# Graph attention on one core: edges laid out as 392 consecutive ones along each partition, with a small stage that joins the partitions afterwards

## The reference, cut to what matters

```python
x = layernorm(x + L0(x, stack([src, dst])))        # 3 layers: gather rows, matmul, relu, segment_sum
q, k, v = x @ Wq + bq, x @ Wk + bk, x @ Wv + bv    # per node, 8 heads of 16
e = edge_attr @ We                                 # per edge, 64 -> 128
k_j, v_j = k[src] + e, v[src] + e
logits = sum(q[dst] * k_j, axis=-1) / sqrt(16)     # per edge and head
m = segment_max(logits, dst)                       # softmax over the edges with one target
ex = exp(logits - m[dst])
alpha = ex / segment_sum(ex, dst)[dst]
agg = segment_sum(alpha * v_j, dst)                # per node, 128
h = ln(agg + x @ Wskip + bskip + x)
x = layernorm(x + ln(gelu(h @ Wf1 + bf1) @ Wf2 + bf2 + h))
```

## Time and profile before

| | us |
|---|---|
| median of the runs | 4584.0 |
| the profiled execution, first to last instruction | 5458.0 |
| attention, first gather to last averaged row | 3201.2 to 4589.7 |

### The profile page before, as it was taken

One profiled execution on the slowest core, in us unless ns is written; L12 is line 12 of the kernel. 1 busy time (PEld: TensorE's weight loads), 2 busy tenths in 40 slices (PEclk: granted clock), 3 DMA queues, 4 the chain that ended last, 5 costly groups with the idle time before them and its releaser, 6 DMA issues. The chain is left out here.

```text
span 5458.0 us, 111849 instructions
## 1 busy us (share of the span) xinstructions
PE 4332.6 (79%) x23759; PEld 2886.3 (53%) x23858; DVE 3587.2 (66%) x12001; ACT 2141.5 (39%) x4806; POOL 2901.1 (53%) x2863
## 2 busy tenths in 40 slices
PE   5666664888867888689999967777777775999998
PEld 2444443666645666556666635555555553444444
DVE  7566653444434444478888847667766765899998
ACT  0222221444433444323333323232323332777777
POOL 0555555555535555354444335555555553777775
PEclk9888887999979999989999977777877777999999
DMA  0333334666646666568888744444544443444443
GB/s 18 125 123 131 127 126 119 189 192 186 188 139 184 188 190 189 172 195 266 266 262 264 241 154 134 131 134 130 143 132 129 135 132 92 117 125 128 126 128 99
DMA packets 693097, 852.73 MB, mean 156 GB/s; under 512 B 149445, under 2 KB 511032, under 8 KB 692916
## 3 DMA queue, kind: packets, MB, share of 16 engines
q1 hardware_dynamic: 580020, 631.94, 35.7%
q0 software_dynamic: 112896, 218.94, 16.7%
HBM read 451.91 MB, written 398.61 MB: 156 GB/s over the span
## 5 line engine op out<-in xcount | busy, mean ns | idle before, releaser
L760 POOL DMA_INDIRECT mp_gathered<-msg_rows,other_idx x784 | 752.4, 960 | 659.0 <-PE bank L776 211.1
L776 PE MATMUL bank<-mp_edge_hot,mp_gathered 128*128 128x256 bf16 x3528 | 539.7, 282 | 203.1 <-issue 166.0
L1066 POOL DMA_INDIRECT ll_gathered<-msg_rows,other_idx x392 | 376.1, 959 | 479.1 <-PE bank L1085 228.8
L526 POOL DMA_INDIRECT by_window<-so_pay,so_pos_i x392 | 397.7, 1015 | 435.5 <-issue 299.0
L1372 POOL DMA_INDIRECT at_kv<-kv_rows,kv_idx x392 | 375.6, 958 | 456.3 <-PE bank L1403 176.4
L776 PEld LDWEIGHTS bank<-mp_edge_hot,mp_gathered 128*128 x3528 | 349.8, 99 | 349.2 <-issue 294.3
L879 DVE TENSOR_TENSOR mp_msg_out<-mp_rest,mp_msg_out 128x256 bf16<-128x256 f32 x392 | 166.8, 425 | 490.5 <-ACT mp_msg_out L837 290.7
L824 ACT ACTIVATE mp_h_out<-bank,mp_b_agg 128x256 f32<-128x256 f32 x392 | 185.8, 474 | 714.5 <-PE bank L794 321.6
L1670 POOL DMA_INDIRECT ff_agg<-at_rows,last_idx x392 | 385.8, 984 | 115.9 <-issue 103.0
L1374 POOL DMA_INDIRECT at_q<-q_rows,node_idx x392 | 371.8, 948 | 130.2 <-issue 130.2
L856 DVE TENSOR_SCALAR mp_edge_hot<-digits,mp_first_col,column 128x256 bf16<-128x256 bf16 x1176 | 346.7, 357 | 80.3 <-issue 62.0
(11 more groups left out here) (258 smaller groups left out, 10199.2 us busy)
## 6 DMA issues: line engine op xcount, KB each, us to landing
msg_rows<-mp_msg_out SPq DMA_DIRECT2D x392, 192.0 KB
mp_h_in<-h_cols SPq DMA_DIRECT2D x392, 128.0 KB
h_cols<-mp_h_out SPq DMA_DIRECT2D x392, 128.0 KB
kv_rows<-ll_proj SPq DMA_DIRECT2D x98, 512.0 KB
msg_rows<-so_msg_out SPq DMA_DIRECT2D x98, 384.0 KB
h_cols<-so_h_out SPq DMA_DIRECT2D x98, 256.0 KB
ll_h_in<-h_cols SPq DMA_DIRECT2D x196, 128.0 KB
x_rows<-ll_x_b SPq DMA_DIRECT2D x98, 256.0 KB
```

The lines of the kernel that those rows point to most:

```text
L526: pool.indirect_dma_start(core.by_window, bass.IndirectOffsetOnAxis(ap=pos_i[k][:, t:t + 1], axis=0), pay[k][:, t, :], None, bounds_check= ...
L760: pool.indirect_dma_start(gathered[:, r * PARTS * D:(r + 1) * PARTS * D], None, core.msg_rows[layer % 2], bass.IndirectOffsetOnAxis(ap=cor ...
L776: product = nc.tensor.matmul(agg_bank[k], gathered[:, bass.ds(at + d * D, D)], hot, start=(first and d == 0), stop=True, skip_group_check= ...
L1066: pool.indirect_dma_start(gathered[:, r * PARTS * D:(r + 1) * PARTS * D], None, core.msg_rows[(LAYERS - 1) % 2], bass.IndirectOffsetOnAxis ...
```

## The change

Partition p now holds edges 392p to 392p+391, and group g is 4 consecutive edges of every partition. So the edges of one target lie along the free dimension without any transpose, and the state is compact: a maximum and a denominator for 8 heads (128 x 8 a step of 4, laid out as 8 x 5 with a slot in front that carries the previous group's value) instead of 128 x 512. The numerator scan is 128 x 640 (128 channels x 5 slots). `factor` holds exp of two gaps (weight and decay) for 8 heads, and ACT spreads the decay to 16 channels. POOL gathers four tiles of keys and values, waiting for `ke_ok`, then four of queries, waiting for `prod_ok`; each kind counts on its own semaphore. PE keeps only the attribute transposes, the product with We (into four PSUM banks in turn, not one) and the skip product (two banks); the fillers are gone. The flags are no longer written and loaded: they are computed once as a table in SBUF (`joins`, and from it `brk` for all groups, 128 x 3920).

The tables of the sort become 128 x 392 tables loaded directly, without four transposes. A target whose edges cross from one partition to the next is not finished by this scan. The new stage `join_runs` gathers each partition's first finished row, carries the ends across the 128 partitions with scans, and scatters the corrected rows back. So rows in `at_rows` are now 144 numbers wide (128 values, 8 maxima, 8 denominators), and `feed_forward` gathers 576 B instead of 512 B a row.

```diff
-        self.at_rows = dram("at_rows", [NP + 1, D], F32)
-        self.same_row = dram("same_row", [1, NP + 1], BF16)
+        self.at_rows = dram("at_rows", [NP + 1 + P, ROW], F32)
...
-                for c, tile in enumerate(parts_f):
-                    for b in range(T):
-                        last = nc.tensor.transpose(bank[c][:, b * P:(b + 1) * P], tile[:, b, :], core.ident[:, :])
+                nc.vector.tensor_tensor(core.joins[:, 1:NT], core.node_idx[:, 1:NT], core.node_idx[:, 0:NT - 1], ALU.is_equal).then_inc(tab, 1)
...
@@ attention, SP @@
-            def load_flags(g, k, i):
-                reached(sp, brk_ok, g - DEEP + 1)
-                sp.dma_start(same[k][:, :], core.same_row[0, bass.ds(g * GR, GR)].partition_broadcast(D)).then_inc(same_in[k], 16)
+                for lo, hi in ((0, SPLIT), (SPLIT, last)):
+                    sp.dma_start(attr[k][lo:hi, :, :], bass.AP(edge_attr.tensor, edge_attr.offset + (lo * NT + g * J) * ED,
+                                                              [[NT * ED, hi - lo], [ED, J], [1, ED]])).then_inc(a_in[k], 16)
+                sp.dma_start(core.at_rows[0:NP, :].rearrange("(p j) f -> p j f", j=NT)[:, g * J:(g + 1) * J, :],
+                             rows[g % DEEP][:, :, :]).then_inc(st[g % DEEP], 16)
@@ attention, POOL @@
-                reached(pool, prod_ok, g - DEEP + 1)
-                reached(pool, ve_ok, g - DEEP + 1)
-                reached(pool, e_mm, g - DEEP + 2)
-                for t in range(T):
...
+                reached(pool, ke_ok, g - DEEP + 1)
+                for t in range(J):
+                    at = g * J + t
+                    pool.indirect_dma_start(kv[g % DEEP][:, t, :], None, core.kv_rows,
+                                            bass.IndirectOffsetOnAxis(ap=core.kv_idx[:, at:at + 1], axis=0)).then_inc(kv_in[g % DEEP], 16)
                 reached(pool, prod_ok, g - DEEP + 1)
+                for t in range(J):
+                    at = g * J + t
                     pool.indirect_dma_start(q[g % DEEP][:, t, :], None, core.q_rows,
+                                            bass.IndirectOffsetOnAxis(ap=core.node_idx[:, at:at + 1], axis=0)).then_inc(q_in[g % DEEP], 16)
@@ attention, ACT @@
+                nc.scalar.activation(factor[k][:, :, :, 1:SLOT].rearrange("p a h j -> p (a h) j"),
+                                     gap[k][:, :, :, :].rearrange("p a h j -> p (a h) j"), ACT.Exp, scale=-SCALE).then_inc(f_ok, 1)
+                nc.scalar.activation(decay[k][:, :, :].rearrange("p (h c) j -> p h c j", h=H),
+                                     factor[k][:, 1, :, :].unsqueeze(2).broadcast_to([P, H, C, SLOT]), ACT.Copy).then_inc(dec_ok, 1)
+                nc.scalar.activation(rows[k][:, :, D:ROW], top_den[k][:, :, :, 1:SLOT].rearrange("p a h j -> p j (a h)"), ACT.Copy).then_inc(state_ok, 1)
@@ attention, DVE @@
             def turn(do):
+                do(0, values)
+                do(-1, weigh)
+                do(0, keys)
+                do(-1, num_scan)
+                do(0, products)
+                do(-1, den_scan)
                 do(0, edge_logits)
-                do(-2, weigh)
-                do(-2, num_scan)
-                do(-2, den_scan)
-                do(-1, maxima)
-                do(-3, divide)
+                do(-1, carry_num)
+                do(-1, inverses)
+                do(0, maxima)
+                do(0, gaps)
+                do(0, carry_top)
+                do(-1, averages)
...
+def join_runs(core):
...
+            pool.indirect_dma_start(firsts[:, :], None, core.at_rows, bass.IndirectOffsetOnAxis(ap=core.run_end[:, 0:1], axis=0)).then_inc(a_in, 16)
+            pool.wait_ge(row_ok, 1)
+            pool.indirect_dma_start(core.at_rows, bass.IndirectOffsetOnAxis(ap=core.run_to[:, 0:1], axis=0), firsts[:, :], None).then_inc(moved, 16)
...
+            nc.vector.tensor_tensor_scan(top[:, 1:1 + P], brk[:, :], z[:, 1, :], 0.0, ALU.add, ALU.max).then_inc(c_ok, 1)
...
+            nc.vector.tensor_tensor_scan(num[:, 1:1 + P], scale[:, 1, :], end_v[:, :], 0.0, ALU.mult, ALU.add).then_inc(c_ok, 1)
```

More of the change, by code:

```diff
@@ new lines, in attention @@
+        brk = sb("break", [P, NG * FLAT])
+        logits, top_den = two("logits", [P, H, SLOT]), two("top_den", [P, 2, H, SLOT])
+        drop, gap = sb("drop", [P, H, J]), two("gap", [P, 2, H, J])
+        factor, decay = two("factor", [P, 2, H, SLOT]), two("decay", [P, D, SLOT])
+        wv, num, inv = two("weighted", [P, D, SLOT]), two("num", [P, D, SLOT]), two("inv", [P, H, J])
+        rows, zero_rows = deep("rows", [P, J, ROW]), sb("zero_rows", [P, ROW])
+        in_run, runs = sb("in_run", [P, NT - 1]), sb("runs", [P, 8])
@@ L1354, in _ @@
+            for n in range(-5, NG + 4):
+                for lag, step in ((5, load), (3, load_cols), (-1, store_skip), (-3, store)):
+                    if 0 <= n + lag < NG:
+                        step(n + lag)
+            sp.wait_ge(zero_st, 32)
             for k in range(DEEP):
@@ L1382, in _ @@
             pe.wait_ge(wts, 16)
-            pe.wait_ge(setup, FILLED + 1)
+            pe.wait_ge(setup, FILLED)
             pe.wait_ge(parts_c, 8)
-            def keep_busy(to):
-                for n in range(4):
-                    nc.tensor.matmul(to[:, :], core.ones[:, :], filler[:, :], start=True, stop=True, skip_group_check=True)
             def turn_attr(g, k, i):
-                pe.wait_ge(a_in[k], 16 * (i + 1))
+                pe.wait_ge(a_in[k], 32 * (i + 1))
                 reached(pe, a_ok, g)
                 pe.nop(nofuse=True)
-                for t in range(T):
+                for t in range(J):
                     last = nc.tensor.transpose(attr_bank[0:ED, t * P:(t + 1) * P], attr[k][:, t, :], ident[:, :])
@@ L1398, in edge_features @@
             def edge_features(g, k, i):
-                reached(pe, prod_ok, g)
-                keep_busy(e_bank)
                 pe.wait_ge(a_ok, g + 1)
-                for t in range(T):
-                    last = nc.tensor.matmul(e_bank[:, t * P:(t + 1) * P], attr_cols[k][:, t * P:(t + 1) * P], w_e[:, :],
+                reached(pe, prod_ok, g - DEEP + 1)
+                for t in range(J):
+                    last = nc.tensor.matmul(e_banks[k][:, t * P:(t + 1) * P], attr_cols[k][:, t * P:(t + 1) * P], w_e[:, :],
@@ L1494, in _ @@
+            def turn(do):
+                do(3, attr_copy)
+                do(0, factors)
+                do(0, decays)
+                do(0, skip_copy)
+                do(-1, states)
             turns(act, turn, DEEP, 8)
@@ new lines, in _ @@
+            joined, length, whole = core.joins[:, 0:1], runs[:, 0:1], runs[:, 1:2]
+            nc.vector.tensor_tensor_scan(in_run[:, :], core.joins[:, 1:NT], core.joins[:, 1:NT], 1.0, ALU.mult, ALU.bypass).then_inc(run_c, 1)
+            dve.wait_ge(run_c, 1)
+            nc.vector.tensor_reduce(length, in_run[:, :], AXX, ALU.add).then_inc(run_c, 1)
+            dve.wait_ge(run_c, 2)
+            dve.wait_ge(based, 2)
+            nc.vector.tensor_scalar(whole, length, float(NT - 1), None, ALU.is_equal).then_inc(run_c, 1)
@@ new lines, in _ @@
+            nc.vector.tensor_tensor(runs[:, 2:3], length, base_f[:, 0:1], ALU.add).then_inc(run_c, 1)
+            dve.wait_ge(run_c, 4)
+            nc.vector.tensor_tensor(core.through[:, :], whole, joined, ALU.mult).then_inc(run_c, 1)
+            nc.vector.tensor_tensor(runs[:, 3:4], runs[:, 2:3], base_f[:, 1:2], ALU.subtract).then_inc(run_c, 1)
+            dve.wait_ge(run_c, 6)
+            nc.vector.scalar_tensor_tensor(out=runs[:, 4:5], in0=runs[:, 3:4], scalar=joined, in1=base_f[:, 1:2], op0=ALU.mult, op1=ALU.add).then_inc(run_c, 1)
@@ new lines, in _, with e_rows, break_of, values @@
+            nc.vector.tensor_copy(core.run_end[:, :], runs[:, 2:3]).then_inc(run_c, 1)
+            dve.wait_ge(run_c, 8)
+            nc.vector.tensor_copy(core.run_to[:, :], runs[:, 4:5]).then_inc(run_c, 1)
+            dve.wait_ge(first_ok, 7)
+            def e_rows(k):
+                return e_banks[k][:, :].rearrange("p (j f) -> p j f", j=J)
+            def break_of(g):
+                return brk[:, bass.ds(g * FLAT, FLAT)]
+            def values(g, k, i):
+                dve.wait_ge(kv_in[k], 64 * (i + 1))
+                dve.wait_ge(e_mm, g + 1)
+                reached(dve, wv_ok, g - 1)
+                nc.vector.tensor_tensor(v_e[k][:, :, :], kv[k][:, :, D:2 * D], e_rows(k), ALU.add).then_inc(ve_ok, 1)
@@ L1870, in build @@
         core.end_stage()
+        join_runs(core)
+        core.end_stage()
         feed_forward(core, l1, out)
```

498 lines of the change are left out of this document (265 added, 233 removed).

## The result

The kernel after took 4680.9 us (median of four runs, 4675.3 to 4683.4), the kernel before on the same chip 4582.9 us (4580.0 to 4588.6): a ratio of 1.0215, with a 95% interval of 1.0201 to 1.023. Forecast were 4535 us and a range of 4420 to 4605. In the text VectorE is DVE of the rows, TensorE PE, GpSimd POOL; SBUF is the memory of the tiles, and PSUM, "bank" in the rows, the one in whose eight banks TensorE's products are put.

A forecast was written before the change was run, and what follows sets the result against it. Attention was taken to be bound by POOL, DVE and PE waiting for each other in a ring, afterwards by POOL's gathers. Timed: attention 1050 - 989, join - 18, sort's head + 6, so 49 us less: 4535 us, range 4420 to 4605.

The forecast's parts named there:

- So POOL never waits and becomes the bound: 980 us: Attention after: POOL's 784 gathers at 1.25 us each, with no waits for buffers, set the time.
- the slower side: Rival, attention: POOL's gathers slowed beside DVE's SBUF copies, 0.35 us a group, 34 us in 98 groups, 4619 us; chance 0.16.
- Timed attention before 1050 us: Attention of the kernel before in timed runs, without the profiled execution's slack: 1050 us, bounds 1000 and 1134.
- VectorE's turn 7.6 us: Attention after: DVE's operations add up to 7.6 us a group, upper bound 10.0.
- TensorE under POOL's time even at 1.2 GHz: Attention after: PE, without fillers, eight transposes and denominators' products, stays under POOL's 10.0 us a group.
- The end of the stage, 9 us behind POOL: Attention after: last queries' landing, 1.8 us, and some 7 us of operations follow POOL's 980, making 989 us.
- The join, 18 us: New stage join_runs, all on the path: adds 18 us, bounds 12 and 28.
- The sort's head, 6 us less: Start of the sort: four transposes, their evictions and the flags' stores leave; 6 us less, bounds 0 and 8.
- Sort, messages and feed forward unchanged: Other stages: message gathers and products stay, and wider rows cost feed forward nothing; no move beyond a few us.
- stalls kept: Rival: the timed attention before stalls as in the profile, 1134 or 1166 us, giving 4451 or 4419 us; chance 0.12.
- faster gathers without the profiler: Rival, attention: POOL's gathers take 1.0 us each without the profiler, so the gain is 137 us, 4447 us; chance 0.15.
- the stage at its floor already: Rival: attention before was already at its floor and nothing else happens, 4585 us; chance 0.07.

The follow-up runs named there:

- e1: The kernel before, unchanged, run for a second profiled execution: 4590.1 us in its one run, span 4588.0.
- e4: The kernel after with its scan split in two, and decay, weigh's factors and reciprocals in PSUM: 4550.4 us, ratio 0.9934 to the kernel before.
- e11: The kernel after without the stage join_runs, that part of the computation left out: 4666.7 us.
- e2: The kernel after with its scan of 128x640 made as two scans of 128x320 over the same memory: 4620.1 us, ratio 1.0078 to the kernel before.
- e8: e4 with four more VectorE copies of 128x512 per group from SBUF to SBUF: 4561.5 us, ratio 0.9949 to the kernel before.
- e12: e4 with one extra scan of 128x512 per group, both operands in SBUF, between values and weigh: 4613.8 us, ratio 1.0054 to the kernel before.

## Why the prediction was wrong

The step that failed is "So POOL never waits and becomes the bound: 980 us". The first half held: no buffer's wait is left. The second half had POOL right and its price wrong, since the sum has nothing for gathers that VectorE holds up. The 980 came of 784 gathers at 1.25 us each, and that length did not stay. From the first gather to the last rows the stage took 1124.3 us, not 989: 135 us too few, for a miss of 146 in all. The gathers that took over 1.0 us (197 of 784) account for 134 of them.

The mechanism stood among the rivals, as the slower side, with POOL's gathers beside VectorE's work in SBUF. It named the wrong operations, the copies, and took 0.35 us per group where 1.4 was measured. Its own full count, three hits a group, was 1.4 us before it took a quarter of that; the agreement is luck, since the three hits were put down to copies (the largest is 0.27 us, L1538), and the late gathers are two a group. The count of operations whose operands both lie in SBUF would have told it: before, one per group that is long (drop, 0.69 us), after, three (1.07 + 1.47 + 1.06 = 3.6 us). The section of the Trainium skill that the rival cited ("SBUF — State Buffer", "Who interferes with whom") has the sentence on two inputs beside the one on copies that I took; and the late gathers of the trace of before, eight in 3400 to 4400 us, all began in that one operation. The mean of the gathers, 957 ns, hid them.

Point by point:
- *Timed attention before 1050 us.* In e1 it is 1035.6 (2682.1 to 3717.7), within the bounds and 14 us off. Reading the slack as gone was right, but the nearness is in part luck: the gathers had none of it left (989.4 us against 980), while the end of the stage, for which the floor had about 20 us, took 46.2. In e4, whose gathers are late only at the stage's start, the stage takes 993.7 us (2671.3 to 3665.0), close to the 989, so 42 us less than before in place of the forecast's 61; 37 of them come from the end of the stage and 5 from the gathers. The layout without late gathers was worth 39 us by the spans (4588.0 to 4548.7) and 35 by the medians of the runs made side by side (4585.6 to 4550.4), to the 49 of the forecast.
- *VectorE's turn 7.6 us.* The operations' records add up to 8.3 and overlap a little; VectorE was busy for 504 / 70 = 7.2 us a group. Weigh and the averages take 1.07 and 1.06 us instead of 0.69; the logits (0.66) take no more for their stride, the scan of 640 takes 1.47 and not 1.58. It was hidden, as said, but the 0.38 us on two of them also made the windows longer in which a gather can be caught.
- *TensorE under POOL's time even at 1.2 GHz.* Right. Its clock was 0.50 from 2800 to 3600 us (0.88 in e1), with 393 us busy in these 800, and nothing waited for it. From feed forward's first gather to the first gelu it was 30.1 us before and after, so the lower clock in the attention cost nothing there either.
- *The end of the stage, 9 us behind POOL.* Right: the last gather ends at 3779.6, the last rows at 3789.1, 9.5 us.
- *The join, 18 us.* 16.3 by the traces of e11.
- *The sort's head, 6 us less.* Counting starts at 14.5 us for 22.6, 8.1 less. Another 9 us are gone by the attention's start, spread over untouched stages; in the ten kernels that are alike up to there (after, e2 to e8, e11, e12) it began between 2664.8 and 2673.6 us, so those 9 us can't be told from scatter.
- *Sort, messages and feed forward unchanged.* Right by e1 and after: 1079.5 and 1073.1 us for the messages (1079.8 in e4, so the 6 us are scatter), 858.6 and 856.9 for feed forward.

Of the other rivals, stalls kept is refuted by e1's 10.1 us per group, and so is faster gathers without the profiler: with that pace in the profiled execution and 2 us between its span and its run, there is nothing for them to explain. The last one, the stage at its floor already, was right of the gathers and not of what follows them. DVE did not become the bound; it was busy for 504 of 800 us in after, 63% and not 75 to 80. Before, it was busy for 743 of 800 (e1).

## What to carry to other kernels

When one engine's indirect gathers are, or become, the bound, list VectorE's long operations beside them and count those whose two inputs are both in SBUF; move one input to PSUM, which cost VectorE nothing here (1.07 and 1.05 us in e4), or cut the operation into short ones. Sort the gathers in the trace by what runs when they start, before trusting their mean. Look at how far the following engine has fallen behind when the last gather ends: that backlog, 46 us here, is paid in full. And where a profiled execution is far longer than its timed runs, take each stage at its bounding engine's floor first, and price a change from there.

## What the hardware showed that I had not expected

- Beside the operations of two inputs and the short copies a gather is held only at its start. One that began 0.22 us before a two-input operation ran through it in 0.95 us, and so did others that began 0.01 to 0.05 us before one; one that began inside waited until 0.19 us (scans) or 0.26 us (weigh) before the record's end. VectorE's operation isn't longer for it: weigh takes 1.07 us in e4 too, where nothing waits.
- One gather does not fit "only at its start". At the head of the stage a query gather began at 2672.59 and took 3.80 us. VectorE's records there are a memset of the break table at 2673.25 (0.71 us) and then a tensor_scalar of it from SBUF to SBUF at 2673.80 (1.77 us), each with at most one input. Less its 0.95 us the gather was let go at 2675.44, 0.13 before that one's end. e4 has the same gather, at 3.90 us; no run takes it apart. So operations with at most one input can hold a gather for longer, 2.85 us, than any with two did here.
- The loop settles on a bad phase by itself. VectorE starts when the last keys and values have landed, some 2 us after the gather's end, so in after weigh and the scan lay under the starts of the same two query gathers in group after group. The same extra scan cost 10 us in one place and 63 in another.
- Weigh and the averages, which write or read 512 numbers in steps of five beside a broadcast operand, take 1.07 us in place of 0.69; the averages of before had the broadcast operand without the steps and took 0.69, and the reduction that writes its 32 numbers in such steps takes 0.66. No run takes the two apart within one operation.
